# Last layernorm's power applied to the head's product, the third stage's low part written across partitions, GpSimd's weight pieces placed in earlier steps

## The reference

```python
def _ln(x, g, b, eps=1e-05):
    mu = x.mean(-1, keepdims=True)
    xc = x - mu
    var = (xc * xc).mean(-1, keepdims=True)
    return xc * jax.lax.rsqrt(var + eps) * g + b
...
    x = x + att @ out_w[i] + out_b[i]
    y = _ln(x, ln2_g[i], ln2_b[i])
    hdn = jax.nn.gelu(y @ ff1_w[i] + ff1_b[i], approximate=False)
    x = x + hdn @ ff2_w[i] + ff2_b[i]
return _ln(x, lnf_g, lnf_b) @ head_w + head_b
...
h = h + _L0_attn_ref(_layernorm(h, axis=-1), ...)
h = h + _L0_ffn_ref(_layernorm(h, axis=-1), ...)
```

## Time and profile before

| | us |
|---|---|
| median of 3 runs (lowest to highest) | 123.97 (123.26 to 125.06) |
| the profiled execution | 122.81 |
| its span, first to last instruction | 121.0 |
| PE busy | 110.0 (91% of the span) |
| DVE busy | 84.0 (69%) |
| ACT busy | 65.0 (54%) |
| POOL busy | 52.6 (43%) |

### The profile page before, as it was taken

How to read it: one execution, slowest core, us unless ns; L and a number is a source line. 1 busy time by engine, 2 the same in 40 slices (tenths; PEclk the granted TensorE clock), 3 DMA queues, 4 the chain that set the end, 5 groups by cost and what they waited for, 6 DMA issues and landing times.

```text
span 121.0 us, 2457 instructions
## 1 busy us (share of the span) xinstructions
PE 110.0 (91%) x914; PEld 99.3 (82%) x914; DVE 84.0 (69%) x251; ACT 65.0 (54%) x148; POOL 52.6 (43%) x62
## 2 busy tenths in 40 slices
PE   6889899999999999999999998599876969999991
PEld 6789799897789889898898886389755968999990
DVE  5000376997999978998799976678798997376002
ACT  4000444685459994899899947354514173521520
POOL 0000256167638752688426966459763230023000
DMA  4999999995900000000000000000000000000202
GB/s 102 355 409 406 405 411 415 409 392 125 363 0 0 0 5 3 0 0 5 0 0 0 5 0 3 3 0 0 5 0 0 0 0 0 0 5 0 65 0 65
DMA packets 4011, 11.97 MB, mean 99 GB/s; under 512 B 448, under 2 KB 1568, under 8 KB 4000
## 3 DMA queue, kind: packets, MB, share of 16 engines
q1 hardware_dynamic: 4000, 11.82, 26.0%
HBM read 11.43 MB, written 0.39 MB: 98 GB/s over the span
## 4 chain that ended last, share of the span: by engine, by line
PE 36%; DVE 25%; ACT 11%; POOL 10%; DMA 7%; issue 5%; SPq 3%; POOLq 0%; DVEq 0%
DMA patches_sb<-in_patches 7%; PE bank L591 6%; PE bank L513 6%; PE bank L373 5%; DVE xn L752 4%; PE bank L488 3%; POOL rstd L1245 3%; ACT kexp L1119 3%; POOL fcw_lo L1303 3%; PE bank L356 2%; SPq L303 2%; PE bank L576 2%; ACT L1147 2%; DVE nkmax L817 2%; DVE stats L737 2%
## 5 line engine op out<-in xcount | busy, mean ns | idle before, releaser
L1245 POOL TENSOR_TENSOR rstd<-mv,minus_half 128x2 f32<-128x2 f32 x14 | 10.2, 731 | 34.6 <-DVE mv L741 34.6
L1119 ACT ACTIVATE kexp<-bank,nkmax 128x256 f32<-128x256 f32 x16 | 7.4, 474 | 6.4 <-DVE nkmax L817 6.4
L1114 ACT ACTIVATE qkvw_hi<-qkvw 128x512 fp32r<-128x512 f32 x6 | 3.5, 623 | 11.5 <-DMA qkvw<-in_qkv_w 11.5
L1264 POOL TENSOR_TENSOR qn<-q,rqsum 128x512 f32<-128x512 f32 x8 | 8.4, 1047 | 2.7 <-DVE rqsum L840 2.7
L373 PE MATMUL bank<-embed_sb,patches_sb 128*128 128x128 f32 x64 | 8.5, 280 | 0.6 <-DMA patches_sb<-in_patches 0.6
L457 PE MATMUL bank<-cw,qT 128*128 128x128 f32 x64 | 8.8, 282 | 0.0
L488 PE MATMUL bank<-restw,hid 128*128 128x128 f32 x64 | 8.1, 280 | 0.6 <-ACT hid L1147 0.6
L373 PE MATMUL bank<-embed_sb 128*128 128x128 f32 x64 | 7.9, 280 | 0.8 <-DMA embed_sb<-in_embed 0.8
L373 PEld LDWEIGHTS bank<-embed_sb 128*128 128x128 f32 x64 | 7.7, 194 | 1.2 <-DMA embed_sb<-in_embed 1.2
L373 PEld LDWEIGHTS bank<-embed_sb,patches_sb 128*128 128x128 f32 x64 | 7.8, 191 | 1.0 <-DMA patches_sb<-in_patches 0.8
L457 PEld LDWEIGHTS bank<-cw,qT 128*128 128x128 f32 x64 | 7.8, 192 | 0.9 <-issue 0.8
(11 more groups left out here) (149 smaller groups left out, 328.8 us busy)
## 6 DMA issues: line engine op xcount, KB each, us to landing
patches_sb<-in_patches SPq DMA_DIRECT2D x4, 512.0 KB, 10.2
embed_sb<-in_embed SPq DMA_DIRECT2D x2, 768.0 KB, 6.5
restw<-in_rest_w SPq DMA_DIRECT2D x2, 768.0 KB, 15.3
embed_sb<-in_embed SPq DMA_DIRECT2D x2, 384.0 KB, 7.8
qkvw<-in_qkv_w SPq DMA_DIRECT2D x3, 256.0 KB, 8.9
qkvw<-in_qkv_w SPq DMA_DIRECT2D x1, 768.0 KB, 16.0
embed_sb<-in_fc_w SPq DMA_DIRECT2D x1, 768.0 KB, 6.9
embed_sb<-in_embed SPq DMA_DIRECT2D x1, 576.0 KB, 4.3
```

The lines of the kernel that those rows point to most:

```text
L1119: nc.scalar.activation(kexp[i][:, c, :], KB[c // 2][:, (c % 2) * TOKENS:(c % 2 + 1) * TOKENS], ACT.Exp, bias=nkmax[i][:, c:c + 1], accum_o ...
L1245: nc.gpsimd.tensor_tensor(rstd[i][:], mv[i][:, :, 1], minus_half[:], ALU.pow).then_inc(rstd_ready[i], 1)
L1264: nc.gpsimd.tensor_tensor(qn[i][:, t, :].rearrange("p (h d) -> p h d", h=HEADS), q[i][:, t, :].rearrange("p (h d) -> p h d", h=HEADS), rqs ...
```

## The change

Three edits. First, LNF's `xn` is only centred (`normf_centre`), without a wait for `rstd`. The head's product is multiplied by `rstd` behind it, in `h_from_head`, tile by tile, which adds `headb`. Since the norm's offset can no longer go in ahead of that multiplication, it goes through the head once: a matmul with the offset as the left side (`offset_through_head`) and one DVE addition (`head_bias`). PE transposes image 0's LNF ahead of `attend(l, i, 1)` of step 3, where it stood behind it.

Second, `xn` of LN3 and LN4 no longer holds the last 64 channels twice; the transposed block has 64 rows, `yT_end`'s first half is copied, and the low part is computed from partitions 0 to 63 and written to partitions 64 to 127.

Third, POOL's pieces move. `mix_fc(0)` goes from step 2's second half to its front, `mix_fc(1)` from step 3 to step 2, `fc_low_part(0)` from the tail to step 3's front, `aqkv_low_part(1)` from the tail to step 3, all `mix_proj` to the tail; step 1's first `qkv1_low_part` now waits for DVE's `yT_lo`. ACT's two `fc` high parts move with them.

```diff
@@ tensor @@
             def turn_norm3(i, n, banks):
-                pe.wait_ge(xn_ready[i], XN[n] + TILES * EPC)
                 for c in range(EPC):
+                    rows = (P, REST)[c]
                     for t in range(TILES):
-                        mm = nc.tensor.transpose(banks[c][:, t * P:(t + 1) * P], xn[i][:, t, c * P:(c + 1) * P], ident)
+                        pe.wait_ge(xn_ready[i], XN[n] + t + 1)
+                        mm = nc.tensor.transpose(banks[c][0:rows, t * P:(t + 1) * P], xn[i][:, t, c * P:c * P + rows], ident)
...
+            def offset_through_head():
+                pe.wait_ge(loaded["head"], 16)
+                offset = col("lnf_b").to_broadcast([P, P])
+                nc.tensor.matmul(KB[1][:, 0:E], offset, headw[:], start=True, stop=True).then_inc(headb_done, 1)
...
                 if s < STEPS - 1:
                     turn_norm1(1 - i, (s + 1) // 2, HALVES)
+                else:
+                    turn_norm(0, LNF, CB)
                 attend(l, i, 1)
-            turn_norm(0, LNF, CB)
+            offset_through_head()
             head(0)
@@ vector @@
-                    if width == E:
-                        nc.vector.tensor_scalar(xn[i][:, t, E:EP], src[:, t, P:E], mv[i][:, t, 0:1],
-                                                rstd[i][:, t:t + 1], ALU.subtract, ALU.mult).then_inc(xn_ready[i], 1)
+            def normf_centre(i):
+                for t in range(TILES):
+                    dve.wait_ge(moments[i], 2 * TILES * LNF + TILES + t + 1)
+                    nc.vector.tensor_scalar(xn[i][:, t, 0:D], x[i][:, t, :], mv[i][:, t, 0:1], None,
+                                            ALU.subtract).then_inc(xn_ready[i], 1)
...
-                    end = yT3_end[i][REST:P, :]
-                    nc.vector.tensor_tensor(end, bankof[REST:P, 0:TOKENS], end.bitcast(F32),
-                                            ALU.subtract).then_inc(yT_lo_ready[i], 1)
+                    nc.vector.tensor_tensor(yT3_end[i][REST:P, :], bankof[0:REST, 0:TOKENS],
+                                            yT3_end[i][0:REST, :].bitcast(F32), ALU.subtract).then_inc(yT_lo_ready[i], 1)
...
+            def h_from_head(i, t):
+                dve.wait_ge(headb_ready, 1)
+                dve.wait_ge(rstd_ready[i], LNF + 1)
                 dve.wait_ge(head_done, i + 1)
...
+                nc.vector.scalar_tensor_tensor(out=h[i][:, t, :], in0=HB[i][:, t * E:(t + 1) * E], scalar=rstd[i][:, t:t + 1],
+                                               in1=headb[:], op0=ALU.mult, op1=ALU.add).then_inc(h_ready[i], 1)
...
             norm_stats(1, LNF, x[1], D, x_new[1], TILES + 1, 1)
+            normf_centre(1)
             phi3_min(0, 0)
-            norm_apply(1, LNF, x[1], D)
             phi3_min(0, 1)
@@ scalar, in the steps @@
+                    fc_high_part(0)
                 if s == 2:
                     act.wait_ge(loaded["aqkv"], 16)
                     weight_high_part("aqkv", aqkvw, aqkvw_parts[0][:])
-                if s >= 2:
-                    act.wait_ge(fc_mixed, s - 1)
-                    weight_high_part("fc", fcw[:, s - 2, :], fcw_parts[0][:, s - 2, :])
-            normf(0, CB)
+                if s == STEPS - 1:
+                    normf(0, CB)
+                    fc_high_part(1)
@@ gpsimd, in the steps @@
                     if s == 1:
+                        pool.wait_ge(yT_lo_ready[1], LOW[LN1(0)])
                         qkv1_low_part(0)
+                    if s == 2:
+                        mix_fc(0)
+                    if s == 3:
+                        fc_low_part(0)
                     rsqrt(ip, LN2(lp))
                     after_norm(ip, LN2(lp))
...
-                    else:
-                        mix_fc(s - 2)
-                        mix_proj(s - 2, s - 1)
+                    if s == 2:
+                        mix_fc(1)
+                    if s == 3:
+                        aqkv_low_part(1)
```

More of the change, by code:

```diff
@@ L285, in build @@
         LOW.update({n: n + 1 for n in range(2 * LAYERS)})
-        XN = {n: TILES * n for n in range(LN3 + 1)}
-        XN[LN4] = XN[LN3] + TILES * EPC
+        XN = {n: TILES * n for n in range(LN4 + 1)}
         HALVES = [SB_, CB]
@@ L753, in norm_apply, with head_bias @@
                                             rstd[i][:, t:t + 1], ALU.subtract, ALU.mult).then_inc(xn_ready[i], 1)
-                    if width == E:
-                        nc.vector.tensor_scalar(xn[i][:, t, E:EP], src[:, t, P:E], mv[i][:, t, 0:1],
-                                                rstd[i][:, t:t + 1], ALU.subtract, ALU.mult).then_inc(xn_ready[i], 1)
+            def normf_centre(i):
[3 more added lines that the diff above has]
+                                            ALU.subtract).then_inc(xn_ready[i], 1)
+            def head_bias():
+                dve.wait_ge(headb_done, 1)
+                dve.wait_ge(loaded["rows"], 16)
+                nc.vector.tensor_tensor(headb[:], KB[1][:, 0:E], rows_sb[:, ROW["head_b"]:ROW["head_b"] + E],
+                                        ALU.add).then_inc(headb_ready, 1)
             def norm1_tile0(i, l, bankof):
@@ L776, in norm3_high @@
                 dve.wait_ge(turned[i], TURNED[n] - EPC + c + 1)
[L777 removed]
+                rows = (P, REST)[c]
+                nc.vector.tensor_copy((yT3_hi, yT3_end)[c][i][0:rows, :], bankof[0:rows, 0:TOKENS]).then_inc(hi3_ready[c], 1)
             def norm3_low(i, n, c, bankof):
@@ L1019, in _ @@
                 close_moments(i, LN2(l), 1, D, 3)
+            head_bias()
             norm_apply(1, LN2(1), x[1], D)
-            h_from_head(0)
-            norm_stats(0, LN3, h[0], E, h_ready[0], 1, 0)
+            for t in range(TILES):
+                h_from_head(0, t)
+            norm_stats(0, LN3, h[0], E, h_ready[0], 1, 1)
             norm2_low(1, 1)
@@ L1037, in _ @@
                 phi3_sum(0, t)
-            h_from_head(1)
-            norm_stats(1, LN3, h[1], E, h_ready[1], 1, 0)
+            for t in range(TILES):
+                h_from_head(1, t)
+            norm_stats(1, LN3, h[1], E, h_ready[1], 1, 1)
             q3_times_k_sum(0)
@@ L1100, in normf @@
                 act.wait_ge(turned[i], TURNED[LNF])
-                nc.scalar.activation(yT[i][:], bankof[:, 0:TOKENS], ACT.Identity, bias=col("lnf_b"),
-                                     scale=col("lnf_g")).then_inc(norm_ready[i], 1)
+                nc.scalar.activation(yT[i][:], bankof[:, 0:TOKENS], ACT.Copy, scale=col("lnf_g")).then_inc(norm_ready[i], 1)
             def norm3_high(i, n, c, bankof):
                 act.wait_ge(turned[i], TURNED[n] - EPC + c + 1)
-                nc.scalar.activation((yT3_hi, yT3_end)[c][i][:], bankof[:, 0:TOKENS], ACT.Copy).then_inc(hi3_ready[c], 1)
+                rows = (P, REST)[c]
+                nc.scalar.activation((yT3_hi, yT3_end)[c][i][0:rows, :], bankof[0:rows, 0:TOKENS],
+                                     ACT.Copy).then_inc(hi3_ready[c], 1)
             def q3_to_sbuf(i):
@@ L1247, in after_norm @@
             def after_norm(i, n):
-                pool.wait_ge(xn_ready[i], XN[n] + TILES * (EPC if n >= LN3 else 1))
+                pool.wait_ge(xn_ready[i], XN[n] + TILES)
             def norm2_low(i, l):
@@ L1267, in normalise_q, with add_bias3 @@
                                         ALU.mult).then_inc(qn_ready[i], 1)
-            def add_bias3(i, row, ready):
-                pool.wait_ge(ready, 1)
+            def add_bias3(i, row, ready, count):
+                pool.wait_ge(ready, count)
                 nc.gpsimd.tensor_tensor(hb[i][:], h[i][:], row.unsqueeze(1).to_broadcast([P, TILES, E]),
@@ L1359, in _ @@
                 rsqrt(1 - i, LN1((s + 1) // 2))
-                after_norm(1 - i, LN1((s + 1) // 2))
-            aqkv_low_part(1)
+                if s < STEPS - 1:
+                    after_norm(1 - i, LN1((s + 1) // 2))
             rsqrt(1, LN2(1))
-            after_norm(1, LN2(1))
-            add_bias(1, "ff2_b", 1, x_mid[1], TILES * LAYERS)
             rsqrt(0, LN3)
             after_norm(0, LN3)
-            fc_low_part(0)
+            add_bias(1, "ff2_b", 1, x_mid[1], TILES * LAYERS)
             fc_low_part(1)
             rsqrt(1, LNF)
-            after_norm(1, LNF)
-            add_bias3(0, b_out, h_ready[0])
-            mix_biases()
-            mix_proj(2, HC)
+            add_bias3(0, b_out, h_ready[0], TILES)
+            mix_proj(0, 2)
             rsqrt(1, LN3)
             after_norm(1, LN3)
-            add_bias3(1, b_out, h_ready[1])
+            mix_proj(2, 4)
+            add_bias3(1, b_out, h_ready[1], TILES)
             rsqrt(0, LN4)
             after_norm(0, LN4)
-            add_bias3(0, projb[:], h2_ready[0])
+            mix_biases()
+            mix_proj(4, HC)
+            pool.wait_ge(mixed_weights, 2)
+            add_bias3(0, projb[:], h2_ready[0], 1)
             rsqrt(1, LN4)
             after_norm(1, LN4)
-            add_bias3(1, projb[:], h2_ready[1])
```

(1 more changed line is left out.)

18 lines of the change are left out of this document (10 added, 8 removed).

## The result

The kernel after takes 124.6 us (median of 6 runs, 124.15 to 124.97), the kernel before, run beside it on the same chip, 123.62 (6 runs, 122.78 to 125.06). The ratio is 1.0096 [1.0061, 1.0131]: slower by about 1 us, within the 2% that I called no change. I had forecast 124.1, between 122.2 and 125.0, as +0.3 on the kernel before; the interval of the ratio shuts +0.3 (1.002) out. The profiled execution took 124.15 us, its span is 122.3.

What follows compares the result with a forecast made beforehand. PE was taken as the bound, with time lost in waits, mainly for DVE. The terms -0.3 + 0.65 + 0.99 - 1.0 = +0.3 us, on before's mean of 123.78, gave 124.1, range 122.2 to 125.0.

Steps and rivals of the forecast that it cites:

- Part 1: POOL's pieces beside DVE's yT_lo in steps 1 to 3, blocking it where they meet: -0.3, +0.65 and +0.99 us.
- Step 1: The new wait puts qkv1_low_part(0) behind yT_lo, returning 0.34 us on DVE, of which -0.3 was taken.
- Step 2: mix_fc(0) at the front blocks yT_lo, which ends at 47.92 in place of 47.27: +0.65 us.
- Step 3: fc_low_part(0) at the front blocks yT_lo, which ends at 62.42 in place of 61.43: +0.99 us.
- The covers: DVE's two maxima hide step 1's rsqrt (otherwise some 0.3); step 2's fc high part has 0.2 us spare.
- Rival (b): Each meeting costs 0.34 us, whatever POOL still has to run: -0.6 in sum, 123.2; chance 0.12.
- Part 2: End of step 3: LNF's transposes delay image 1's attention product by some 0.2; net +0.06 for PE at 80.58.
- Part 3: LNF of image 1, in the tail: early centring moves transposes by -0.6, h by -0.3, attend3(0) by -0.54 us.
- Part 4: LN3 and LN4: each norm about 0.46 shorter, LN4's transposes of image 0 1.0 earlier; tail in all -1.0 us.
- rival (c): The low part written across partitions is slow: 124.1 + 2e, with e extra each; chance 0.03.
- the granted clock is 1.00 in both, so time is lost in waits: Windows of steps and tail, PE busy 9.80 and 8.02 of 10 us: lost time put down to waits alone.
- rival (d): The tail gives nothing, since each early xn meets another late one: +1.3, 125.1; chance 0.09.

Runs made afterwards that it cites:

- e4: Kernel before with only the third edit (moved POOL and ACT pieces, new wait of step 1): 124.66 us, ratio 1.0085.
- e2: Kernel after with POOL's moved pieces put back where they were, the wait of step 1 kept: 122.73 us, ratio 0.9921.
- e9: Kernel before plus an unread POOL addition of two SBUF operands ahead of rsqrt in steps 2 and 3: 123.72 us, ratio 1.0047.
- e10: Kernel before plus three unread, write-only POOL fills ahead of rsqrt in steps 2 and 3: 123.31 us, ratio 0.9992.
- e1: Kernel after plus five unread matmuls in PE's two tail pauses, around the transposes of image 1's LN2: 123.49 us, ratio 1.0009.
- e5: Kernel before with only the second edit (64-row transposes, low part across partitions, shorter norms): 122.19 us, ratio 0.9919.
- e11: Kernel after unchanged, run once more to count executions with the lower clock: 124.06 us, ratio 1.0008 to before.
- e3: Kernel after with POOL's pieces back in their old places and unread matmuls in the two tail pauses: 121.68 us, ratio 0.9863.
- e12: Kernel after with POOL's pieces back, image 0's LNF transposes behind the attention product, seven unread matmuls in PE's pauses: 121.34 us, ratio 0.9859.
- e8: Kernel before plus four unread matmuls, two ahead of the first head and two ahead of the last ff1: 123.1 us, ratio 0.9972.

## Why the prediction was right, and where it was not

**Part 1, the meetings: right, term by term.** Step 1 was given 0.34 on DVE and 0.35 came back (0.77 to 0.42). Step 2 was given 0.65: `mix_fc(0)` ends at 47.25, `yT_lo` at 47.53, 0.28 later, its length up by 0.63. Step 3 was given 0.99: POOL ends at 62.37, `yT_lo` at 62.66, its length up by 0.98. The covers held as named: `rsqrt` follows the moved `qkvw_lo` at 34.06 with no delay behind it, and ACT's `fc` high part (47.28, 0.84 long) ends 0.97 before the exponentials. e4 measures the whole at +1.3, e2 its absence, e9 and e10 the mechanism. Rival (b), the bare 0.34, falls by the lengths; a blocked operation costs what POOL still has to run.

**Part 2: mis-sized by 0.1.** +0.06 was given for 80.58, with 0.2 of delay ahead of LN2 of image 1 in it; up to LN2, from 71.11 (the last step's context, 69.89 before, so +1.22) to 78.43 (+1.39) it is +0.17. What I had seen as one delay of 0.2 had a second side that I did not price: PE's work ahead of that point is gathered before `xn`, and what is left is one pause of 1.12 us. At 80.58 itself the fall hides the reading. In e1, which has none, these transposes stand at +1.10, counted from the first `yT_lo`, against +1.24 at the context: -0.1 there, where +0.06 was given.

**Part 3: right in the wait, wrong in who gains.** LNF's transposes came 0.68 earlier relative to what precedes them (2.44 to 1.76; 0.6 was given), `h` 0.60 (2.44 to 1.84; 0.3 was given), and `attend3(0)` 0.66 (2.44 to 1.78; 0.54 was given). e1, without a fall, gives the same 0.66 for the first and the last. The sizes are near, the cause that I named for the first two is not what the end hangs on: I credited the early centring of edit 1, and e5, which has none of it, yields the same 0.29 ahead of `attend3(0)` and the whole 1.0. What of edit 1's gain ends in the wait for `qzT` was not tried by itself.

**Part 4: right.** LN4's transposes idle 0.21 in place of 0.94, and the tail behind the fall of the clock gives 2.44 - 1.34 = 1.10 (1.0 was given). The low part across partitions takes 0.42, as the ordinary one beside it does (0.41 at 83.90); rival (c) has nothing. From `turn_q3(1)` to the end the length is unchanged, +1.34 and +1.3.

**Where it was not right: "the granted clock is 1.00 in both, so time is lost in waits".** It is true of the two windows and of the profiled execution, and it hid that the kernel before falls to 1.2 GHz in 35 of 91 executions. The forecast named four of the tail's waits; 0.75, 0.24 and 0.75 us ahead of 78.37, behind which the clock falls, and 0.65, 0.65 and 0.39 behind 89 are not in its list. The sum has no term for a pause that costs more than its own length, and no rival for it. In the profile of after this is 1.05 us (+1.39 at 79.76 to +2.44 at 85.22). Without it the terms come to what they were given: +0.1 in e1's profile, +0.3 and +0.5 in the medians at full clock of e1 and e11, +0.3 forecast.

**What was luck.** The measured +1.0 is three times the +0.3, and by its size nearer to rival (d), "the tail gives nothing", +1.3. That rival is wrong all the same: the tail gave 1.1 back, and the fall took about as much. All six of the first runs of after were lower, against seven of twelve in e11. And 124.1 was a sum on a mixture: before's mean of 123.78 is made of times from 122.81, at a full clock, to 125.06, which is above every full-clock execution of before on record (124.17 at most). On a full-clock base the same +0.3 would have read 0.5 to 0.8 lower.

**What stays open.** Why one execution falls and the next, of the same kernel, does not. Filling the pauses matters (0 of 12 in e1 against 9 of 12 in e2, same group). How the fall's share depends on their lengths is not settled: 13 of 18 and 9 of 12 with 1.1 and 0.75 us, 4 of 12 with 0.33, 0.33 and 0.75, 3 of 10 in e4 with 0.75, 0.31 and 0.75, and e1's result cannot say which of its two pauses decides. Whether the kernel after falls more often than before is not shown: 13 of 18 against 35 of 91 over all groups, but 7 of 12 against 14 of 29 in the one group that has both. So how much of the first +1.0 belongs to the change, and how much to six executions that all happened to fall, is open too.

## What to carry to other kernels

Before moving a GpSimd operation, look whether it reads SBUF and whether a DVE operation with two SBUF inputs on the critical path will start inside it: the price is all that GpSimd still has to run plus a short restart (0.28 us behind its end, operation included, with 128 x 256 here), and the same operation a few hundred nanoseconds off costs nothing. Read the granted clock of many executions, not of the profiled one, compare executions at the same clock, and look at TensorE's longest pauses: one can cost 1 us behind it, beside its own length. Where such pauses can't be shortened, matmuls that nobody reads made the fall rare here (1 of 24 executions in e1, e3 and e12) at no measurable price, but only at the pauses where they stand (e8).
